# A fused two-layer block on Trainium2: another order of the work behind the last chunk of the time mixing stage

## What is computed

```python
xk, xv, xr = (x * tm + xs * (1 - tm) for tm in (tm_k, tm_v, tm_r))   # xs: x one token back
k, v, r = xk @ Wk.T, xv @ Wv.T, sigmoid(xr @ Wr.T)
wkv = _wkv(time_decay, time_first, k, v)       # a scan over tokens, per channel
ln = (wkv - mean) * rsqrt(var + eps) * ln_g + ln_b      # over the channels
s = (r * ln) @ Wo.T
x = x + s * silu(ffn)
xn = layernorm(x)          # input of layer 1
```

## Time and profile before

| | us |
|---|---|
| median of 3 runs | 2266.08 |
| lowest, highest | 2265.18, 2269.56 |
| profiled execution, its own time | 2264.35 |
| its span, first to last instruction | 2262.6 |
| mean granted TensorE clock, share of full speed | 0.899 |

### The profile page before, as it was taken

One profiled execution on the slowest core, in us unless ns is written; L12 is line 12 of the kernel. 1 busy time (PEld: TensorE's weight loads), 2 busy tenths in 40 slices (PEclk: granted clock), 3 DMA queues, 4 the chain that ended last, 5 costly groups with the idle time before them and its releaser, 6 DMA issues. The chain is left out here.

```text
span 2262.6 us, 34573 instructions
## 1 busy us (share of the span) xinstructions
PE 1862.6 (82%) x10272; PEld 1514.9 (67%) x10272; DVE 1249.9 (55%) x2155; ACT 794.6 (35%) x1666; POOL 893.5 (39%) x644
## 2 busy tenths in 40 slices
PE   3399999999999698894536883786699999997996
PEld 2189999999999333342215662676598899985775
DVE  5145555555555588987418311355365666564887
ACT  3122222222222245643203110234366666662121
POOL 0512121121211254445205275021577777773554
PEclk7589999999999898997768896787899999998998
DMA  6420101010111401222380013200478887885564
GB/s 221 173 77 29 57 28 56 28 56 28 46 38 48 155 20 55 70 79 80 118 310 28 1 48 109 110 1 1 172 276 278 278 281 280 284 283 199 180 207 149
DMA packets 97647, 279.17 MB, mean 123 GB/s; under 512 B 13506, under 2 KB 15136, under 8 KB 94240
## 3 DMA queue, kind: packets, MB, share of 16 engines
q1 hardware_dynamic: 80320, 228.29, 28.9%
q0 software_dynamic: 17248, 49.86, 6.7%
HBM read 210.39 MB, written 67.71 MB: 123 GB/s over the span
## 5 line engine op out<-in xcount | busy, mean ns | idle before, releaser
L619 DVE TENSOR_TENSOR rffn_h<-rffn_ps_hidden,rffn_silu 128x128 f32<-128x128 f32 x272 | 79.4, 292 | 301.4 <-ACT rffn_silu L592 301.4
L592 ACT ACTIVATE rffn_silu<-rffn_ps_hidden 128x128 f32<-128x128 f32 x272 | 75.6, 278 | 458.7 <-PE rffn_ps_hidden L667 458.7
L628 DVE TENSOR_TENSOR rffn_y<-rffn_ps_y,rffn_y 128x512 f32<-128x512 f32 x272 | 188.0, 691 | 3.0 <-PE rffn_ps_y L686 1.1
L667 PE MATMUL rffn_ps_hidden<-rffn_w0h,rffn_xsh 128*128 x544 | 156.7, 288 | 7.3 <-issue 4.6
L561 POOL TENSOR_TENSOR rffn_w1l<-rffn_raw,rffn_w1h 128x768 fp32r<-128x768 f32 x32 | 59.2, 1851 | 254.4 <-ACT rffn_w1h L581 254.4
L667 PE MATMUL rffn_ps_hidden<-rffn_w0h,rffn_xsl 128*128 x544 | 154.5, 284 | 0.0
L667 PE MATMUL rffn_ps_hidden<-rffn_w0l,rffn_xsh 128*128 x544 | 153.9, 283 | 0.0
L667 PE MATMUL rffn_ps_hidden<-rffn_w1h,rffn_xsl 128*128 x544 | 153.9, 283 | 0.0
L667 PE MATMUL rffn_ps_hidden<-rffn_w1h,rffn_xsh 128*128 x544 | 153.6, 282 | 0.0
L667 PE MATMUL rffn_ps_hidden<-rffn_w1l,rffn_xsh 128*128 x544 | 153.1, 281 | 0.0
L561 POOL TENSOR_TENSOR rffn_w0l<-rffn_raw,rffn_w0h 128x768 fp32r<-128x768 f32 x32 | 58.8, 1840 | 221.2 <-ACT rffn_w0h L581 221.2
(11 more groups left out here) (618 smaller groups left out, 5905.9 us busy)
## 6 DMA issues: line engine op xcount, KB each, us to landing
moe_raw<-in_moe_w SPq DMA_DIRECT2D x47, 769.5 KB
moe_raw<-in_moe_w SPq DMA_DIRECT2D x47, 768.0 KB, 5.4
rffn_raw<-in_ffn_w SPq DMA_DIRECT2D x16, 1536.0 KB, 6.8
ys<-moe_y SPq DMA_DIRECT2D x47, 512.0 KB
xs<-route_zero SPq DMA_DIRECT2D x17, 256.0 KB
rffn_x_in<-xs SPq DMA_DIRECT2D x17, 256.0 KB, 3.1
ys<-rffn_y SPq DMA_DIRECT2D x17, 256.0 KB, 2.0
y<-in_x SPq DMA_DIRECT2D x4, 1024.0 KB
```

The lines of the kernel that those rows point to most:

```text
L592: nc.scalar.activation(sil[n % 2][:], hb[n % 2][:, 0:P], ACT.Silu).then_inc(s_sil, 1)
L619: nc.vector.tensor_tensor(h32[n % 2][:], hb[n % 2][:, P:GU], sil[n % 2][:], ALU.mult).then_inc(s_h32, 1)
L628: nc.vector.tensor_tensor(y[:, t, :], yb[n % 2][:], y[:, t, :], ALU.add).then_inc(s_yadd, 1)
L667: last = nc.tensor.matmul(hb[n % 2][:], xs[p][:, c, t * P:(t + 1) * P], w[j][q][:, bass.ds(mine + c * GU, GU)], start=(c == 0 and m == 0), ...
```

## The change

`walk` now ends at step 15. What followed is written out for each engine as one list. In it DVE does `sums(15)`, `low(6)`, `divide(14)` and `divide(15)` before `gate_out(8)`; POOL does `quotient(15)` first, then `gather(11)`, which stood in step 15 ahead of the gate of block 2 and whose silu moves with it; SP, ACT and PE get orders that go with these. In the gate of the last block POOL keeps the first half and DVE takes the second (semaphore `last_half_gated`). The turned tiles 8 to 15 go to four banks, the two key and the two value banks, one after the other, and a turn of tile 12 to 15 waits for the `low` of the tile four back, the last reader of its bank. In all blocks, `mean` waits chunk by chunk, `variance` half by half (behind both halves of the centring), and the first `output` of a block half by half of the gate.

```diff
+        s_gd = a.sem("last_half_gated")
...
+        LAST = TPB * (TB - 2)
+        def turned(j):
+            return tx if j < LAST else (kp[0], vp[0], kp[1], vp[1])[j % 4]
         def need(eng, sem, n):
...
         def walk(step):
-            for s in range(STEPS + 2 * KC + 2):
+            for s in range(STEPS):
...
             walk(step)
+            store_parts(6)
+            store_x1(8)
+            load_rows(10)
+            store_x1(9)
+            load_rows(11)
+            store_parts(7)
+            store_x1(10)
+            load_rows(12)
+            store_x1(11)
+            load_rows(13)
+            for j in range(8, 12):
+                store_rows(j)
+                store_parts(j)
+            for j in range(12, NT):
+                store_x1(j)
+                if j + 2 < NT:
+                    load_rows(j + 2)
+                if j >= 13:
+                    store_rows(j - 1)
+                if j >= 14:
+                    store_parts(j - 2)
+            store_parts(14)
+            store_rows(15)
+            store_parts(15)
...
-            def gate(b):
-                for h in range(2):
+            def gate(b, halves=(0, 1)):
+                for h in halves:
...
-                    elif c >= 2:
+                    elif c == 2 or (c == 3 and b < TB - 1):
             walk(step)
+            quotient(STEPS - 1)
+            gather(11)
+            for j in range(8, 12):
+                add_x(j)
+            gather(12)
+            gate(TB - 1, (0,))
+            for j in range(13, NT):
+                gather(j)
+            for j in range(12, NT):
+                add_x(j)
         def _(dve):
...
             def low(j):
                 dve.wait_ge(s_hi, j + 1)
-                nc.vector.tensor_reduce(keep.sums[:, :, 2 * j:2 * j + 2], tx[:]
+                src = turned(j)[:].rearrange("p (c n) -> p c n", n=P) if j >= LAST else tx[:]
+                nc.vector.tensor_reduce(keep.sums[:, :, 2 * j:2 * j + 2], src
-                nc.vector.tensor_tensor(part[j % 2][LO][:], tx[:], f32(part[j % 2][HI][:]), ALU.subtract)\
+                nc.vector.tensor_tensor(part[j % 2][LO][:], src, f32(part[j % 2][HI][:]), ALU.subtract)\
...
             walk(step)
+            b = TB - 1
+            sums(STEPS - 1)
+            low(6)
+            divide(STEPS - 2)
+            divide(STEPS - 1)
+            gate_out(8)
+            gate_out(9)
+            centre(b)
+            moments(8)
+            moments(9)
+            low(7)
+            gate_out(10)
+            norm(b)
+            gate_out(11)
+            invert(4)
+            row_norm(8)
+            dve.wait_ge(s_aff, KC * b + 4)
+            dve.wait_ge(s_rg, KC * b + 4)
+            nc.vector.tensor_tensor(wkv[b % 2][:, 2:4], wkv[b % 2][:, 2:4], r[b % 2][:, 2:4], ALU.mult).then_inc(s_gd, 1)
+            row_norm(9)
+            moments(10)
+            moments(11)
+            low(8)
+            invert(5)
+            row_norm(10)
+            low(9)
+            row_norm(11)
+            gate_out(12)
+            low(10)
+            gate_out(13)
+            low(11)
+            moments(12)
+            gate_out(14)
+            moments(13)
+            invert(6)
+            row_norm(12)
+            gate_out(15)
+            row_norm(13)
+            moments(14)
+            low(12)
+            moments(15)
+            invert(7)
+            row_norm(14)
+            low(13)
+            row_norm(15)
+            low(14)
+            low(15)
         def _(act):
...
             def high(j):
                 act.wait_ge(s_t, j + 1)
-                nc.scalar.copy(part[j % 2][HI][:], tx[:]).then_inc(s_hi, 1)
+                src = turned(j)[:].rearrange("p (c n) -> p c n", n=P) if j >= LAST else tx[:]
+                nc.scalar.copy(part[j % 2][HI][:], src).then_inc(s_hi, 1)
             def step(s, b, c):
...
-                    for t in range(TPB):
+                    for t in range(TPB if b < TB - 1 else TPB - 1):
             walk(step)
+            high(6)
+            silu(11)
+            high(7)
+            squares(TB - 1)
+            std(TB - 1)
+            row_std(4)
+            affine(TB - 1)
+            row_std(5)
+            high(8)
+            high(9)
+            for j in range(12, NT):
+                silu(j)
+            high(10)
+            high(11)
+            row_std(6)
+            high(12)
+            row_std(7)
+            high(13)
+            high(14)
+            high(15)
         def _(pe):
...
-            def average(src, sem):
+            def average(src, sem, ready):
                 for k in range(KC):
+                    ready(k)
                     last = nc.tensor.matmul(mq[:], mean_w[:], src[:, k, :], start=(k == 0), stop=(k == KC - 1))
...
             def mean(b):
-                pe.wait_ge(s_wkv, KC * (b + 1))
-                average(wkv[b % 2], s_mean)
+                average(wkv[b % 2], s_mean, lambda k: pe.wait_ge(s_wkv, KC * b + k + 1))
             def variance(b):
-                pe.wait_ge(s_sq, 2 * b + 2)
-                average(sq, s_var)
+                pe.wait_ge(s_ctr, 2 * b + 2)
+                average(sq, s_var, lambda k: pe.wait_ge(s_sq, 2 * b + k // 2 + 1))
             def output(j):
-                if t == 0:
-                    pe.wait_ge(s_gt, 2 * b + 2)
-                    if j == 0:
-                        pe.wait_ge(s_w[O_], 16)
+                if j == 0:
+                    pe.wait_ge(s_w[O_], 16)
                 if t < 2:
...
                 for k in range(KC):
+                    if t == 0 and k % 2 == 0:
+                        if k and b == TB - 1:
+                            pe.wait_ge(s_gd, 1)
+                        else:
+                            pe.wait_ge(s_gt, 2 * b + k // 2 + 1)
                     last = nc.tensor.matmul(ro[t % 2][:], wkv[b % 2][:, k, t * P:(t + 1) * P], w[O_][:, k, :],
...
                 pe.wait_ge(s_y, j + 1)
-                need(pe, s_lo, j)
+                need(pe, s_lo, j if j < LAST else j - 3 if j >= LAST + 4 else 0)
+                out = turned(j)[:].rearrange("p (c n) -> p c n", n=P) if j >= LAST else tx[:]
-                    last = nc.tensor.transpose(tx[:, c, :], y[j % 2][:, c * P:(c + 1) * P], ident[:])
+                    last = nc.tensor.transpose(out[:, c, :], y[j % 2][:, c * P:(c + 1) * P], ident[:])
...
             walk(step)
+            turn(7)
+            mean(TB - 1)
+            output(10)
+            variance(TB - 1)
+            output(11)
+            turn(8)
+            turn(9)
+            output(12)
+            output(13)
+            turn(10)
+            turn(11)
+            output(14)
+            output(15)
+            for j in range(12, NT):
+                turn(j)
 def top4_router(nc, A, keep, idx_dram):

```

## The result

The changed kernel takes 2227.3 us (median of 4 runs, 2225.89 to 2228.16) against 2265.63 for the kernel before, measured with it (2264.55 to 2269.56): a ratio of 0.9825, 95% interval 0.9807 to 0.9842, 38.3 us less. The forecast was 2226, in a range of 2216 to 2243. The profiled execution took 2228.12 us, with a span of 2226.3.

A forecast was written before the change was run, and what follows sets the result against it. It took the stretch behind the last chunk as bound by a chain of hand-overs, no engine full. 4.6 + 23 + 9 + 3 = 39.6, rounded to 40, off the profiled 2264.35 gave 2224.35, as median 2226 us; range 2216 to 2243.

The forecast's parts named there:

- my case: The main forecast, 2226 us, from 2218 to 2233 for term B, Term A and the port rule; chance 0.60.
- term B: Up to the last division: DVE no longer waits for output(8), so the division ends 21.5 to 24.4 us earlier; taken as 23.
- Term A: Gates of blocks 0 and 1: first outputs start on the first gate half, saving 4.6 us; bounds 0 and 2 × 3.9.
- rival 2: More than the sum: shorter pauses in blocks 0 and 1 keep PE's clock, no collisions; 2221 down to 2217; chance 0.15.
- the collisions: Before the last division, scans, product and gate get in each other's way: four meetings at 0.5 to 1.5 us each.
- Term C: From the last division to the last block's gate: 21.5 us instead of 30.5, a saving of 9.
- Term D: From the last block's gate to the last low: 30.2 us instead of 33.8, a saving taken as 3.
- The cold PE (1): Behind 1040 us, shorter bursts leave PE at its low clock: 14.5 us lost, 2240 us; chance 0.12.
- The late waits (3): Tiles 12 to 15 wait longer for loads, stores and POOL: 9 us lost, 2235 us; chance 0.10.
- Slower stages behind (4): The next stage, begun 40 us earlier, runs more at the low clock: 60 us lost, 2286 us; chance 0.03.
- The time between the halves: Last block's gate: a shared port makes both halves run in turn, gate ready at 1077.8 instead of 1075.9; sum 38.

The follow-up runs named there:

- e6: The changed kernel with divide(14) ahead of sums(15) and low(6) on DVE; median 2223.64 us.
- e11: The kernel before with step 16 alone reordered: both last divisions ahead of gate_out(8) on DVE, quotient(15) ahead of add_x(8) on POOL; median 2251.5 us.
- e8: The kernel before with the new lists of all engines alone: one bank for turns, last gate on POOL, whole waits; median 2237.58 us.
- e4: The changed kernel with both halves of the last gate on POOL; median 2224.47 us.
- e7: The changed kernel with SP's list alone changed: rows of tiles 9 to 11 ahead of parts 8 to 10, load_rows(14) ahead of parts(10); median 2221.37 us.
- e12: The changed kernel measured again unaltered; median 2225.89 us, ratio 0.9834 to the kernel before.
- e9: The changed kernel with both last gate halves on POOL, divide(14) ahead of sums(15), and rows ahead of parts in SP's list; median 2222.66 us.
- e10: e9 with moments(12) and gate_out(13) moved ahead of low(10) on DVE; median 2221.01 us, ratio 0.9795 to the kernel before.

## Why the prediction was right

The sum was 39.6 and the landmarks say 39.3. The chain of waits was right, term by term; that the sum is so close is luck, as the terms missed by +3.0, -2.4, +0.3 and -1.2 us and cancel. The range of my case, 2218 to 2233, is also wider below than its three reasons allow: term B at 24.4 gives 2225, and nothing named leads further down.

**Term A** was put at 4.6 with 7.8 as the upper bound, and it is 7.6 by the two first profiles (6.6 at least). The step that was mis-sized is the clock, which I had left to the bound and to rival 2: PE keeps its clock where its pause shrinks enough. In block 1 the first output began after a pause of 1.39 us instead of 3.47. The windows of the two kernels in which it begins (before, then changed):

```profile
968.00:972.00 4.00, 3.44 (x4) 1.51 (x5) 3.05 (x4) 3.94 (x6) 0.50 (x1) 0.50 0.01 2
```

```profile
964.00:968.00 4.00, 3.41 (x8) 1.42 (x9) 4.00 (x3) 3.88 (x7) 2.49 (x2) 1.00 0.02 4
```

Before, it ran at the low level, 1.2 GHz; now at the high one, 2.4 GHz. So PE does not work at half speed "after every pause", as the prediction has it. In block 0 the pause shrank from 4.21 to 1.96 us and the output still began at the low level (granted 0.50 from 887 to 889), but the high one came back sooner (mean 0.73 instead of 0.50 from 888 to 892). DVE waits nothing for `gate_out(4)`, where it waited 4.16 us; in block 0, 0.76 instead of 3.86. My term counted the half gate whole and the clock not at all. That the finer waits of mean and variance give nothing in blocks 0 to 2 held: DVE waits 0.71 us for the mean of block 1 and 2.17 for that of block 2, in both kernels.

**Term B** was put at 23, and it is 55.10 - 34.46 = 20.6, just under my bound of 21.5. The step that fell short is the collisions, taken at 0.5 to 1.5 us each: copy and scan together lost 4.1 us to POOL's gate (2.30 and 3.32 us, where they took 0.26 and 1.28 before). e6 shows it by taking them out of the gate's way, which gives 3.1 of it back. The move of `gather(11)`, which I had counted as pure gain, is what brought the gate there (e11). The cause itself, DVE standing before output(8) with the last chunk behind it, is shown by e11, with the qualification that the gain was kept only where PE, ACT and SP got new lists as well (e8).

**Term C** was 9 and is 9.3 (30.5 before; 1051.57 to 1072.71 now, 21.1). The order was as worked out, the distances in part by luck. The affine steps ended 16.4 us after the last division, 1.5 sooner than worked out, and two operations ahead of POOL's half lost 1.1 of that: `row_norm(8)` beside `add_x(11)` took 1.52 us instead of 0.54, and `gather(12)` beside DVE's half of the gate 1.70 instead of 1.02 (as in e4):

```profile
1066.84 1.52 DVE L1110 TENSOR_SCALAR mix_y<-mix_g,mix_mv,mix_istd 128x512 f32<-128x512 f32 x1
...
1068.63 1.70 POOL L958 DMA_INDIRECT mix_g<-ys,pos  x1 [0.55 <-DVE mix_y L1110]
```

The two gate halves did not run side by side, which I had named as a sign: DVE's ran from 1068.29 to 1069.50, POOL's from 1070.35 to 1072.71. And the part of it that I had ascribed to sharing the gate does not exist: e4 without it is 1.5 us faster. I had seen that POOL's half would be the late one and not drawn the conclusion.

**Term D** was 3 and is 1.8 (33.8 before, 1072.71 to 1104.76 now, 32.0). The waits for load(14) (4.85 us on POOL) and for the stored parts of tile 13 (ACT; 1.5 us left on DVE) are there as foreseen. Missed was `row_norm(11)`, which waits 4.46 us for rows(9), queued on SP behind parts(8); e7 shows it. So the last low part ended at 1104.76, where I had named 1102.

**The rivals.** The cold PE (1) did not come: the variance and outputs 10 and 11 ran at 3.6 us per four matmuls, the mean at 2.9 for its first three, and only outputs 8 and 12 began cold. The late waits (3) came in part and are in term D. Slower stages behind (4): 1117.4 us instead of 1115.0 in the two profiles, within the 1111.4 to 1120.0 that unaltered stages show. The first part of the next stage, up to the first instruction on `kv_bar`, did take 2.4 us more (251.4 against 249.0, over the 2 us that I had set as a sign; 249.9 in e12), but up to `moe_carrier` it was 449.2 against 450.3, at the same clock of 0.79. The time between the halves, by which I gave 38 instead of 40, was not lost there: `row_norm(9)` ran before POOL's half in 0.54 us. The collisions fell on `row_norm(8)` and the gather ahead of the halves, and above all at the start of the list.

## What to carry to other kernels

At the end of a software pipeline the steady order of each engine can be the wrong one: look for the wait whose queue holds work that does not depend on it, and move that work ahead, on every engine whose list it crosses, SP's among them. Look, too, at what a moved operation will then run beside: here an earlier gate met a scan and took back 3 us. A wait split by halves is worth more than its half where TensorE's pause shrinks enough to keep its clock. Splitting a step over two engines gained nothing here, as the later half was queued behind other work, and cost about 1.5 us.

## What the hardware showed that I had not expected

- A VectorE copy of 128×2 elements took 2.30 us instead of 0.15 to 0.26 beside a GpSimd product over 128×1024, in all eight kernels in which `sums(15)` meets the gate of block 2 and in none of the others (at one other place it took 1.54 in every kernel, beside another GpSimd operation, at 837.88 in the changed one); a 128×512 scan 3.32 instead of 1.28. A reciprocal of 128×512, one input, took its usual 3.34 us beside the same product.
- An indirect DMA's issue on GpSimd took 1.70 us beside VectorE's half of the gate, and 0.94 to 1.3 elsewhere. Three such gathers issued within 3.5 us of each other took longer to reach their silu, 5.6 to 6.0 us for the last (e4, e7, e9, e10), than the one issued by itself in the changed kernel, 3.4.
- The stages behind time mixing, which no kernel of the study alters, varied by 8.6 us between profiles (1111.4 to 1120.0), more than several edits are worth.
